# Cross attention on one NeuronCore: maxima in 32-row tiles of two heads, scores in 64-row tiles

## The reference

```python
ci = rms_norm(hidden_states, ln_post_cross_w)
cq = heads(ci @ cq_w, NH, CHD)                       # NH = 16, CHD = 8
ck, cv = jnp.split(encoder_outputs @ ckv_w, 2, axis=-1)
ck, cv = (heads(ck, NH, CHD), heads(cv, NH, CHD))
# sdpa, without a causal mask:
scores = jnp.einsum('bhqd,bhkd->bhqk', q * scale, k)  # 256 queries, 1601 keys
p = jax.nn.softmax(scores.astype(jnp.float32), axis=-1)
cctx = jnp.einsum('bhqk,bhkd->bhqd', p, v)
hidden_states = hidden_states + cctx @ cdense_w
```

## Time and profile before

| | |
|---|---|
| median of 3 runs | 2678.3 us (2676.37 to 2683.85) |
| profiled execution | 2683.99 us, span 2682.2 us |
| PE busy | 2143.2 us (80%) |
| DVE busy | 1572.0 us (59%) |
| ACT busy | 851.2 us (32%) |
| granted TensorE clock, mean | 0.876 of full |
| layer-2 cross attention from the first maxima step to the copy of the last group's result, first batch | 454.5 to 588.9 us |

### The profile page before, as it was taken

The page is one execution under the profiler, slowest core; times in us unless marked ns, Lnnn a source line. Parts: engine busy times, 40 slices in busy tenths (PEclk is TensorE's granted clock), DMA queues, the critical chain, the costliest instruction groups (busy, mean ns, idle before and its releaser), DMA issues.

```text
span 2682.2 us, 37982 instructions
## 1 busy us (share of the span) xinstructions
PE 2143.2 (80%) x12540; PEld 1575.9 (59%) x12540; DVE 1572.0 (59%) x2513; ACT 851.2 (32%) x1530; POOL 467.2 (17%) x412
## 2 busy tenths in 40 slices
PE   4999776878599977687859997768876999686987
PEld 3677565546477666554747766655464776565545
DVE  6777346653677735665377763566437776355643
ACT  2444111441244412054124441205412443120531
POOL 2444010000244401000034440100003443010000
PEclk7999877899699988798969998869896999886988
DMA  4000101001000010100100001010011000101000
GB/s 153 13 4 32 67 1 71 1 1 40 30 9 4 32 67 1 71 1 1 40 29 9 4 32 67 1 71 1 1 40 30 9 4 32 67 1 71 1 1 4
DMA packets 15563, 74.54 MB, mean 28 GB/s; under 512 B 2096, under 2 KB 3760, under 8 KB 11952
## 3 DMA queue, kind: packets, MB, share of 16 engines
q1 hardware_dynamic: 14256, 68.90, 6.9%
q10 hardware_dynamic: 1152, 3.67, 0.3%
HBM read 71.51 MB, written 1.05 MB: 27 GB/s over the span
## 4 chain that ended last, share of the span: by engine, by line
PE 72%; DVE 17%; issue 7%; ACT 3%; DMA 1%; POOL 0%; DVEq 0%; SPq 0%; ACTq 0%; POOLq 0%
PE x L623 26%; PE st L623 22%; PE pv L623 18%; PE mi L623 4%; DVE rstd_work L1142 1%; DVE prob_sums L1425 1%; DVE max_parts L1245 1%; PE x L642 1%; DVE k_hi_lo L1142 1%; DVE recip_sum L1296 1%; DVE cq_blocks L1480 1%; DVE rstd_work L1201 1%; ACT probs L508 1%; ACT k_hi_lo L466 1%; DVE max_parts L1472 1%
## 5 line engine op out<-in xcount | busy, mean ns | idle before, releaser
L508 ACT ACTIVATE probs<-st 128x512 f32<-128x512 f32 x416 | 229.6, 596 | 385.3 <-PE st L623 380.6
L1472 DVE TENSOR_REDUCE max_parts<-x 128x1 f32<-128x832 f32 x256 | 253.8, 1021 | 109.2 <-PE x L623 107.6
L1245 DVE TENSOR_REDUCE max_parts<-x 128x1 f32<-128x832 f32 x256 | 258.7, 1017 | 54.6 <-PE x L623 53.2
L602 ACT ACTIVATE probs<-st 128x512 f32<-128x512 f32 x416 | 226.3, 596 | 189.0 <-PE st L623 186.4
L623 PE MATMUL st<-q_hi_hi,k_hi_lo 128*128 128x256 f32 x832 | 236.8, 315 | 28.9 <-ACT v L474 14.3
L431 POOL TENSOR_TENSOR prob_sums<-prob_sums,probs 128x512 f32<-128x512 f32 x160 | 205.6, 1285 | 250.0 <-ACT probs L508 250.0
L623 PE MATMUL pv<-probs,v 128*64 128x256 f32 x1664 | 223.2, 393 | 0.0
L623 PEld LDWEIGHTS st<-q_hi_hi,k_hi_lo 128*128 128x128 f32 x832 | 160.7, 193 | 104.2 <-issue 68.4
L623 PE MATMUL st<-q_lo_shift,k_hi_rows 128*128 128x256 f32 x832 | 213.1, 287 | 0.0
L395 POOL TENSOR_SCALAR k_hi_rows<-probs,const_cols 64x1664 fp32r<-64x1664 f32 x16 | 26.4, 1658 | 996.1 <-DVE probs L1209 995.8
L1142 DVE TENSOR_TENSOR prob_sums<-prob_sums,probs 128x512 f32<-128x512 f32 (+1 forms) x168 | 155.2, 924 | 75.0 <-ACT probs L528 42.9
(11 more groups left out here) (260 smaller groups left out, 4405.8 us busy)
## 6 DMA issues: line engine op xcount, KB each, us to landing
w_gate_up<-in_wgu SPq DMA_DIRECT2D x4, 3072.0 KB, 10.5
w_pair<-in_w SPq DMA_DIRECT2D x32, 256.0 KB, 2.7
w_ff<-in_w SPq DMA_DIRECT2D x8, 1024.0 KB, 5.8
w_qk<-in_wqk SPq DMA_DIRECT2D x4, 2048.0 KB, 9.1
w_down<-in_wdn SPq DMA_DIRECT2D x4, 1536.0 KB, 13.8
w_dense<-in_wd SPq DMA_DIRECT2D x4, 1024.0 KB, 12.5
mask_ints<-in_mask SPq DMA_DIRECT2D x4, 832.0 KB, 4.6
ctx_t_raw<-in_ctxT SPq DMA_DIRECT2D x4, 832.0 KB, 6.2
```

Source lines behind the costliest of these rows:

```text
L508: act.activation(prob[:, kt % 4], ST[kt % 2][:], ACT.Exp, scale=HD0 ** -0.5).then_inc(p_exp.handle, 1)
L602: act.activation(prob[:, n % 4], ST[n % 2][:], ACT.Exp, scale=float(HC2) ** -0.5)\
L1245: dve.tensor_reduce(mxs[:, qt, h, half:half + 1], X[half][:].rearrange("p (c n) -> p c n", c=2)[:, :, 0:QUART], AX.XY, ALU.max).then_inc(m ...
L1472: dve.tensor_reduce(mxs[:, qt, h, half:half + 1], X[half][:].rearrange("p (c n) -> p c n", c=2)[:, :, 0:QUART], AX.XY, ALU.max).then_inc(m ...
```

## The change

In the maxima pass a step n now covers two heads (duo = n % 2 gives heads 2 duo and 2 duo + 1) and one quarter c of the keys (416). Each of its two matmuls takes only the 32 rows of its own head, as a 32-row tile of the array, and writes into its own bank of X[duo]. DVE reduces each bank to one value and so writes two values in each step into a new small tile `mxc` of 2 x 4 x 4; the final maximum goes over four quarters in place of two halves. In the second pass the two score matmuls of a key tile take rows 0 to 63 and 64 to 127, as 64-row tiles, each into its own bank of ST as before. The rows left out are zero in the query blocks, so the results are the same. The number of matmuls, their columns, their place in PE's order, and all waits stay as they were; the DVE step reads the same 832 values.

```diff
--- before.py
+++ after.py
@@ -169,6 +169,7 @@
         mv = sb("mean_var", [P, TT, 2])
         rs = sb("rstd_work", [P, 5, TT])
         mxs = sb("max_parts", [P, 2, 4, 2])
+        mxc = sb("max_cross", [P, 2, 4, 4])
         nmx = sb("neg_max", [P, 2, 4])
         rec = sb("recip_sum", [P, NT])
         acc = sb("prob_sums", [P, 2, 512])
@@ -1026,14 +1027,16 @@
                 def cross_max(gr, n):
 
                     i = b * 4 + gr
-                    half, h, qt = n % 2, n // 2 % 4, n // 8
+                    duo, c, qt = n % 2, n // 2 % 4, n // 8
                     if n < 2:
                         pe.wait_ge(ks_read.handle, ks_read.at(i))
                         pe.wait_ge(qg_read.handle, qg_read.at(i))
                     pe.wait_ge(mc2_read.handle, mc2_read.at(i, max(0, n - 1)))
-                    for ch in range(2):
-                        o = half * HALF + ch * QUART
-                        m = mm(X[half][:, ch * 512:ch * 512 + QUART], qb2[gr % 2][:, h, qt * P:(qt + 1) * P], ks2[gr % 2][:, o:o + QUART])
+                    for u in range(2):
+                        h = 2 * duo + u
+                        r = slice(32 * h, 32 * h + 32)
+                        m = mm(X[duo][:, u * 512:u * 512 + QUART], qb2[gr % 2][r, h, qt * P:(qt + 1) * P],
+                               ks2[gr % 2][r, c * QUART:(c + 1) * QUART])
                     m.then_inc(mc2_mm.handle, 1)
 
                 for j in range(2):
@@ -1071,8 +1074,9 @@
                         for u in range(2):
                             n = 2 * kt + u
                             pe.wait_ge(pc_exp.handle, pc_exp.at(i, max(0, n - 1)))
-                            m = mm(ST[n % 2][:], ks2[gr % 2][:, kt * P:(kt + 1) * P],
-                                   qb2[gr % 2][:, 2 * u:2 * u + 2].rearrange("p h n -> p (h n)"))
+                            r = slice(64 * u, 64 * u + 64)
+                            m = mm(ST[n % 2][:], ks2[gr % 2][r, kt * P:(kt + 1) * P],
+                                   qb2[gr % 2][r, 2 * u:2 * u + 2].rearrange("p h n -> p (h n)"))
                             m.then_inc(sc_mm.handle, 1)
                         if gr < 3 and kt == 0:
                             cross_stacks(gr + 1, 0)
@@ -1467,12 +1471,12 @@
 
                 def cross_max(gr):
                     for n in range(16):
-                        half, h, qt = n % 2, n // 2 % 4, n // 8
+                        duo, c, qt = n % 2, n // 2 % 4, n // 8
                         dve.wait_ge(mc2_mm.handle, mc2_mm.at(b * 4 + gr, n + 1))
-                        dve.tensor_reduce(mxs[:, qt, h, half:half + 1], X[half][:].rearrange("p (c n) -> p c n", c=2)[:, :, 0:QUART],
-                                          AX.XY, ALU.max).then_inc(mc2_read.handle, 1)
+                        dve.tensor_reduce(mxc[:, qt, 2 * duo:2 * duo + 2, c], X[duo][:].rearrange("p (u n) -> p u n", u=2)[:, :, 0:QUART],
+                                          AX.X, ALU.max).then_inc(mc2_read.handle, 1)
                     dve.wait_ge(mc2_read.handle, mc2_read.at(b * 4 + gr))
-                    dve.tensor_reduce(nmx[:], mxs[:], AX.X, ALU.max, negate=True).then_inc(nmc.handle, 1)
+                    dve.tensor_reduce(nmx[:], mxc[:], AX.X, ALU.max, negate=True).then_inc(nmc.handle, 1)
 
                 def cross_shifts(gr):
                     dve.wait_ge(nmc_t.handle, nmc_t.at(b * 4 + gr))
```

## The result

The changed kernel takes 2718.78 us (median of 4 runs, 2707.19 to 2730.31) where the kernel before takes 2681.07 (4 runs beside it): 1.0135 times, interval 1.0113 to 1.0156. It is slower by about 38 us; the forecast was 38 us faster. The profiled execution took 2723.48 us, span 2721.7, 39.5 us more than the one of before.

A forecast was written before the change was run, and what follows sets the result against it. VectorE waited for TensorE; with overlapping streams, VectorE's reads would become the bound. Savings of 26 + 11 + 3 + 2, less 4 for the clock, gave 38 us off the 2678.3 median: 2640 us, range 2614 to 2686.

The forecast's parts named there:

- A: The forecast case: matmul streams overlap and VectorE's reads become the bound, 2640 us, own range 2618 to 2655; chance 0.60.
- D: Rival: shorter streams keep the grant at 1.2 GHz; 2666 us (group 0 only, chance 0.06) or 2755 (all groups, 0.03).
- (5): Clock at group starts: TensorE streams less around the 1.86 us stall, so 3 added drops of the grant, 4 us lost.
- (1): Beats of two key tiles in groups 0 to 2: 3.60 us falls to 3.2, 26 us off over 66 beats.
- near 25: Sign to look for: the second pass of a group goes from 27.6 us to about this many us.
- The change of shape: One more switch of tile shape per key tile with maxima, 0.1 us for each added change, ends 0 and 0.2.
- Step (2): Maxima pass of group 0 at 1.2 GHz: shorter waits for matmul pairs, 2.8 us per batch, 11 us off in all.
- (3): First scores of a group: 0.4 us in each of 4 groups 0, 0.15 in each of 8 others, 3 us off.
- (4): Group 3, held by exponentials: at most 0.1 us per key tile, 48 of them, taken as 2 us off.
- VectorE's two results: Two results written per maxima read in place of one, priced at nothing; at 0.05 us each, 10 us given back.

The follow-up runs named there:

- both in 64-row tiles: Changed kernel with maxima steps of heads h and h + 2 in 64-row tiles, like its scores: 2657.29 us, ratio 0.9897 to the kernel before.
- the scores alone: Kernel before with only its scores in 64-row tiles, maxima steps left at 128 rows: 2686.46 us against 2684.71, ratio 1.0007.

## Why the prediction was wrong

1. **Which case.** The forecast gave A, overlap with VectorE as the bound, 0.60, and the clock (D) 0.09 in all. D is what happened: its sign to look for, a grant of 0.50 in windows of the loops, is there. Its price fits too: 2.4 us was forecast for a key tile at 1.2 GHz, 2.38 was measured. Its cause was put as "a step that streams half as long keeps the grant at 1.2 GHz", and that falls short: with scores of 128 rows the same steps keep 1.00, and mostly without overlap 32 rows lose it in one group of three. Its total for all groups, 2755, has a slip: it takes 192 key tiles, which is the number of reads, where 11 in each of 12 groups make 132. With these it is 0.6 x 132 = 79 us, and 2719. That this is the measured time is partly luck, since only eight of twelve loops were lost.

2. **The step that failed is (5), the clock**, put at 4 us. The twelve passes, where (1) and (5) together had 22 us off, took 42.8 us more. The argument against D failed. It was that group 3's loop, thin in streams, ran at 0.92 on average. That loop has no 32-row tiles, and even after the change it ran at full grant behind its first key tiles (1.00 from 594.7 us in the first batch). It says nothing of how a loop with them comes through its first key tiles. The rows of before held a warning that was priced only as "3 such drops, 4 us": the grant goes at group starts. The term left out was coming back. Before, a loop that enters at 0.50 is back within two or three key tiles; with 32-row maxima beside 64-row scores it fell and came back that soon in three of the twelve loops, and in eight only with the last key tile or not at all; there a loss costs 6 to 9 us, not 1.5. Why these tiles keep it away stays open.

3. **Step (1), the beat**, was right at full grant. The one pass of the changed kernel that is at 1.00 throughout takes 25.8 us, and 25.0 is reached with both in 64-row tiles, against "near 25" forecast. Its reads come in beats of 3.07 and 3.42 us in turn, 3.24 on average against the 3.2 taken:

```profile
2554.70 2.89 DVE L1476 TENSOR_REDUCE max_cross<-x 128x2 f32<-128x832 f32 x3 [0.18 <-PE x L624]
...
2558.12 2.89 DVE L1476 TENSOR_REDUCE max_cross<-x 128x2 f32<-128x832 f32 x3 [0.53 <-PE x L624]
```

VectorE still idles 0.18 and 0.53 us for PE, so it is near the bound and not the whole of it.

4. **The change of shape** was sized at 0.1 us, with 0.2 as its end, and reads 0.19 to 0.20 in the rows of the scores alone. That is about the whole second score stream of 0.23, and it eats the gain there. Both in 64-row tiles, one shape for scores and maxima, reach the lowest beat.

The Trainium skill's page "TensorEngine Tiling (Array Packing)", Key Properties, says that a change of tiling mode drains the engine. The trace agrees in sign, with 0.19 to 0.20 us more for maxima behind scores of other rows; that a drain is what this time pays for is not shown.

5. **Step (2), the front pass**, was put at twice what it gave: 2.8 us per batch forecast, 1.35 measured (5.4 in four; 22.84 us in place of 24.2). The pairs did shrink to 0.72 us at the low grant, but VectorE then reads four steps in a row, 3.82 us, before the projection is through, and the rest of the beat is the projection. A beat takes 6.17 us in place of 6.36.

6. **Steps (3) and (4)** can't be read apart from the clock: group 3 went from 98.3 to 103.1 us in four batches, by a lower grant at its start. **VectorE's two results** cost nothing, as taken.

## What to carry to other kernels

Judge a change to matmul shapes by the clock it leaves behind as well as by the time it frees: tiles with few rows can be quicker at full clock and lose that clock at the next stop. Look at where a loop starts, after a wait, and keep full tiles there; the narrow ones can follow. And try neighbouring matmuls with the same rows: here what a change of rows cost was nearly what the overlap of two streams gave.

## What the runs showed of the hardware that was not expected

- Two edits that are harmless alone (0 and -28 us) cost 34 to 38 us together: the clock is at one of two levels, and what each edit leaves of it doesn't add up.
- A loop can run at either level of the clock for its whole length: with the same instructions a pass took 25.8 us at 1.00 and 36.6 at 0.50. Added matmuls of 128 rows and 512 columns, with PE's row 97% full, did not bring it back for 74 us.
- Four float32r matmuls of 32 rows and 416 columns in four banks take as long as two (0.72 and 0.71 us at 1.2 GHz).
- What stays open: what in the array's work the chip goes by. The runs show that 32 rows against 64, with streams of like length, are 51 us apart (2708.45 and 2657.29), but not why groups 0, 1 and 2 of one kernel differ so regularly, nor why the same group is lost in three batches and kept in the fourth. The moment at which a group's first tiles fall may count as well, and each experiment moved that too; no run holds it fixed.
